# Last expert feed-forward of a four-layer block: from all experts for every token to blocks of tokens sorted by expert

## What is computed

```
h = xn * rsqrt(mean(xn * xn) + eps) * norm_w          # xn is the layer norm of x
logits = h @ gate_w.T + gate_b
vals, idx = top_k(logits, 2);  wts = softmax(vals)
t1 = einsum('td,efd->tef', h, mlp1_w) + mlp1_b        # 8 experts, 2 x 128 columns each
glu = min(t1[..., ::2], 7);  lin = clip(t1[..., 1::2], -7, 7)
act = glu * sigmoid(1.702 * glu) * (lin + 1)
y = einsum('tei,edi->ted', act, mlp2_w) + mlp2_b
out = xn + sum over the 2 chosen experts of y * wts
x = x + tanh(g_ffn[3]) * out
```

## Time and profile before

| | us |
|---|---|
| three runs | 1872.49, 1875.36, 1875.47 (median 1875.36) |
| the profiled execution, its own time | 1866.39 |
| its span, first to last instruction | 1864.6 |
| `feed_forward3`: from the last tile of the last attention (1595.3) to the end of the span | 269.3 |
| busy over the span: PE / DVE / ACT / POOL | 1517.3 / 1345.4 / 780.6 / 642.2 |
| mean granted TensorE clock | 0.918 |

### The profile page before, as it was taken

The page is one execution under the profiler, slowest core; times in us unless marked ns, Lnnn a source line. Parts: engine busy times, 40 slices in busy tenths (PEclk is TensorE's granted clock), DMA queues, the critical chain, the costliest instruction groups (busy, mean ns, idle before and its releaser), DMA issues. The chain is left out here.

```text
span 1864.6 us, 33511 instructions
## 1 busy us (share of the span) xinstructions
PE 1517.3 (81%) x10824; PEld 920.6 (49%) x10824; DVE 1345.4 (72%) x3512; ACT 780.6 (42%) x1314; POOL 642.2 (34%) x649
## 2 busy tenths in 40 slices
PE   3788885378989799889889898944789899778877
PEld 1455453145555465555555555522355556445444
DVE  5667776666566537888888888876565656698998
ACT  1555563145656423333333433421356556333333
POOL 0223220012221003353444453454123220477786
PEclk9989997589999899999999999975989999798999
DMA  7543540244344000000000000003053432000000
GB/s 171 68 70 47 73 63 1 34 136 74 48 62 62 1 1 1 7 1 7 6 1 6 0 7 18 1 0 74 0 75 46 67 52 36 1 1 12 11 12 12
DMA packets 62835, 63.59 MB, mean 34 GB/s; under 512 B 6065, under 2 KB 57777, under 8 KB 62129
## 3 DMA queue, kind: packets, MB, share of 16 engines
q1 hardware_dynamic: 62704, 61.99, 20.3%
HBM read 22.12 MB, written 2.10 MB: 13 GB/s over the span
## 5 line engine op out<-in xcount | busy, mean ns | idle before, releaser
L1225 DVE TENSOR_REDUCE neg_max<-bank 128x4 f32<-128x512 f32 x384 | 259.5, 687 | 128.9 <-PE bank L856 126.8
L670 ACT ACTIVATE probs<-bank 128x512 f32<-128x512 f32 x384 | 229.1, 597 | 239.1 <-PE bank L879 236.8
L1026 PEld LDWEIGHTS bank<-room,area 128*128 128x128 f32 x2048 | 249.4, 196 | 100.0 <-issue 62.9
L1026 PE MATMUL bank<-room,area 128*128 128x128 f32 x2048 | 259.8, 281 | 32.0 <-DVE area L1499 18.3
L746 ACT ACTIVATE work<-bank 128x512 f32<-128x512 f32 (+1 forms) x192 | 114.5, 596 | 355.0 <-PE bank L1051 349.9
L439 POOL TENSOR_SCALAR rstd_a<-meanvar 128x4 f32<-128x4 f32 x64 | 16.9, 265 | 676.8 <-DVE meanvar L1181 676.8
L854 PE MATMUL bank<-mask_b,ident_b 128*128 128x512 bf16 x384 | 159.4, 415 | 70.5 <-DVE neg_max L1225 56.7
L1055 PE MATMUL bank<-xT,room 128*128 128x512 f32 (+1 forms) x384 | 200.6, 605 | 15.7 <-DVE area L1499 15.5
L1051 PE MATMUL bank<-xT,room 128*128 128x512 f32 (+1 forms) x384 | 198.4, 599 | 0.0
L1499 DVE TENSOR_TENSOR area<-work,bank 128x512 f32<-128x512 f32 (+1 forms) x192 | 128.8, 679 | 94.5 <-PE bank L1055 74.4
L568 POOL TENSOR_TENSOR prod<-mask_i,work 128x128 f32<-128x128 f32 (+3 forms) x128 | 126.4, 1020 | 154.6 <-DVE mask_i L1560 154.6
(11 more groups left out here) (167 smaller groups left out, 2481.9 us busy)
## 6 DMA issues: line engine op xcount, KB each, us to landing
q_rows<-area SPq DMA_DIRECT2D x144, 128.0 KB
k_rows<-area SPq DMA_DIRECT2D x288, 64.0 KB
ctxT<-ctx_t SPq DMA_DIRECT2D x24, 256.0 KB, 7.7
mask_i<-mask SPq DMA_DIRECT2D x8, 256.0 KB, 8.6
work<-ctx_in SPq DMA_DIRECT2D x8, 256.0 KB, 2.8
out<-x SPq DMA_DIRECT2D x4, 512.0 KB, 3.2
room<-w_down SPq DMA_DIRECT2D x1, 1536.0 KB, 13.4
room<-w_gate SPq DMA_DIRECT2D x1, 1408.0 KB, 6.3
```

The costliest lines, as they stand in the source:

```text
L670: act.activation(probs[j].rearrange("p a b -> p (a b)"), T_BANK[j % 2][:], ACT.Exp).then_inc(exp_done, 1)
L1026: mm = pe.matmul(dst[:, t * P:(t + 1) * P], h[:, t * P:(t + 1) * P], w, start=i == 0, stop=i == len(terms) - 1)
L1225: dve.tensor_reduce(neg_max[:, 4 * j:4 * j + 4], S_BANK[j % 2][:].rearrange("p (h k) -> p h k", h=4), AX.X, ALU.max, negate=True).then_inc ...
```

## The change

The 32 tiles are taken as 4 chunks (`NCH`) of 8 tiles (`TC`), 1024 tokens. Each token of a chunk has two rows, one for each chosen expert. Its two rows are written to a region of the DRAM tensor `moe_rows`, sorted by expert, each expert starting at a multiple of 128 rows; a region has 24 blocks of 128 rows, since 2048 rows of 8 experts need at most 23. Then the blocks are processed, four at a time (`QUAD`), so 6 steps a chunk and 24 in all, numbered k below. Each block has one expert.

- **DVE** per chunk: `choose(c)` (13 small operations: the two experts of each of 8 tiles) and `put(c)` (19: the row number of each token and the expert of each block, as integers, and the two weights). PE counts in between, in `ranks(c)`: 17 bf16 matmuls with a triangle and with ones.
- **POOL** per chunk: 16 indirect transfers of 128 rows of 512 bytes out of `h_all` to `moe_rows` (`scatter`, 8 for each half chunk) and 16 back (`gather`) into `y_taken`. The products move to DVE, `h` too (it is kept for all 32 tiles, `h_all`).
- **SP** loads step k with one transfer of four blocks at a fixed address (`load`, four buffers) and stores the result over it (`store`). It clears `moe_rows` before `token_attention`, in 4 transfers of 1.5 MB.
- **PE** per step: turn the four blocks, multiply by the expert's `mlp1`, whose column in `room` comes from a register (`value_load`, one number for four experts, then shifts), add the bias by a second matmul of a one-hot column with the bias in three bf16 parts, turn the product, multiply by `mlp2` in the same way.
- **DVE** per step: two clamps from PSUM and a product (`gated`), a second product after the sigmoid (`hide`). Per chunk, `combine3` adds the 16 gathered tiles to `x`, times their weights.
- **ACT** per step: copy the turned blocks, the sigmoid, copy the turned product, copy the result.
- At the start one more 64 KB constant is loaded and cast. `load_experts3` loads the biases after the last token attention, since they lie in its buffer.

The core of the diff:

```diff
+TC = 2 * TG
+NCH = NT // TC
+QUAD = 4
+NQ = 6
 ...
             def load_experts3():
                 sp.wait_ge(x_written, NT * 4)
                 sp.dma_start(wr3[:], gate3).then_inc(experts_loaded, 16)
 ...
+                sp.wait_ge(tok_written, NT)
+                sp.dma_start(bias_f[BIAS_ROWS], bias3).then_inc(experts_loaded, 16)
+
+            def feed_forward3():
 ...
+                def load(k):
+                    if k % NQ == 0:
+                        sp.wait_ge(scattered[k // NQ], 16 * 2 * TC)
+                    if k >= 4:
+                        sp.wait_ge(blk_turned, k - 3)
+                    waits_apart(sp)
+                    sp.dma_start(blk[k % 4], moe_rows[k * GT:(k + 1) * GT].rearrange("(j p) d -> p j d", p=P)
+                                 ).then_inc(blk_loaded[k % 4], 16)
 ...
+                for k in range(NCH * NQ):
+                    load(k)
+                    if k >= 4:
+                        store(k - 4)
 ...
+                def scatter(c, half):
+
+                    pool.wait_ge(placed, c + 1)
+                    pool.wait_ge(h3_ready, 2 * c + half + 1)
 ...
+                    for t in range(TG):
+                        for k in range(2):
+                            o = 2 * (TG * half + t) + k
+                            pool.indirect_dma_start(
+                                moe_rows, bass.IndirectOffsetOnAxis(place_i[:, c, o:o + 1].bitcast(mybir.dt.uint32), 0),
+                                h_all[:, TC * c + TG * half + t, :], None).then_inc(scattered[c], 16)
+
+                def gather(c):
+
+                    for b in range(2):
+                        pool.wait_ge(blk_stored[b], 16 * NQ // 2 * (c + 1))
+                    if c >= 2:
+                        pool.wait_ge(combined, c - 1)
 ...
+                for c in range(3):
+                    scatter(c, 0)
+                    rms_norm(2 * c + 3)
+                    scatter(c, 1)
+                    if c < 2:
+                        rms_norm(2 * c + 4)
+                gather(0)
+                scatter(3, 0)
+                scatter(3, 1)
+                for c in range(1, NCH):
+                    gather(c)
 ...
+                    four = pe.value_load(expert_i[0:1, c, q:q + 1], min_val=0, max_val=E ** QUAD - 1)
+                    for j in range(QUAD):
+                        weights_at[k, j] = pe.snap(((four >> 3 * j) & (E - 1)) * (3 * P))
 ...
+                for k in range(NCH * NQ):
+                    c, q = divmod(k, NQ)
+                    turns = min(2 * c + 4 + (q >= 2) + (q >= 4), 2 * NCH)
+                    if k + 1 < NCH * NQ:
+                        turn_blk(k + 1, turns if q < NQ - 1 else min(2 * c + 6, 2 * NCH))
+                    up(k)
+                    if c < 2 and q in (1, 3):
+                        turned(2 * c + 4 + (q == 3), k + 2)
+                    if k >= 1:
+                        turn_hidden(k - 1)
+                    if k >= 2:
+                        down_blk(k - 2)
+                    if c < 2:
+                        if q == 3:
+                            logits(c + 2)
+                        if q == 5:
+                            ranks(c + 2)
 ...
+                for k in range(NCH * NQ):
+                    c, q = divmod(k, NQ)
+                    gated(k)
+                    if c < 2:
+                        if q == 0:
+                            group_norm(2 * c + 5)
+                        if q == 1 and c == 0:
+                            group_stats(6)
+                        if q == 4:
+                            choose(c + 2)
+                        if q == 5:
+                            put(c + 2)
+                            if c == 0:
+                                group_norm(6)
+                                group_stats(7)
+                    hide(k)
+                    if c >= 2 and q == NQ - 1:
+                        combine3(c - 2)
+                combine3(2)
+                combine3(3)
```

More of the change, by code:

```diff
@@ new lines, in program @@
+        chosen = small((2 * TC + 1) * E, BF16).rearrange("p (o e) -> p o e", e=E)
+        rank = small(2 * TC * E).rearrange("p (o e) -> p o e", e=E)
+        place = small(2 * TC)
+        place_i = small(NCH * 2 * TC, I32).rearrange("p (c o) -> p c o", c=NCH)
+        weight = small(NCH * 2 * TC).rearrange("p (c k t) -> p c k t", c=NCH, k=2)
+        blocks_of, ends, begins = small(E), small(E), small(E)
+        blocks_i = small(E, I32)
+        below = small(E * E).rearrange("p (e f) -> p e f", e=E)
@@ L513, in feed_forward3 @@
-                rms_norm(0)
-                def body(gp, first, last):
-                    for gr, b, is_first, left in groups(gp, first, last):
-                        for e in range(E):
-                            if e >= 1:
-                                hide(E * gr + e - 1, e - 1, DB3 + 9 * gr + e - (1 if e >= 3 else 2))
-                            elif not is_first:
-                                hide(E * gr - 1, 7, DB3 + 9 * gr - 2)
-                            if e == 1 and left >= 1:
-                                rms_norm(gr + 1)
-                            products(E * gr + e, e)
@@ L1607, in norm_apply, with group_stats, group_norm @@
+                def group_stats(p):
+                    norm_stats(p, NT * 5 + TG * (p + 1))
+                def group_norm(p):
                     norm(p, 56 + p)
                     dve.wait_ge(xn_ready, XN3 + p + 1)
[L1609 to L1613 removed]
```

481 lines of the change are left out of this document (334 added, 147 removed).

## The result

The changed kernel takes 1921.2 us (median of 4 runs, 1918.3 to 1924.7), the kernel before 1873.9 us beside it (4 runs, 1863.6 to 1875.5): a ratio of 1.0265, with an interval of 1.0237 to 1.0294. It is slower by 47 us, where 12 us less were forecast.

A forecast was written before the change was run, and what follows sets the result against it. DVE was taken to bound the last stage, PE close behind. Seven terms along the chain through DRAM summed to 257.3 us against 269.3, 12.0 less, so 1863.4 us for the median; range 1838 to 1932.

The forecast's parts named there:

- 1, to the first scatter: Last stage's start until the first chunk's row numbers: statistics, norms, logits, `choose`, `ranks`, `put`; 26.0 us.
- 2, scatters, landing, load: First chunk's sixteen scatters (20.3 us) with a 3.65 norm between halves, landing 2.15, load 2.9; 29.1 us.
- 3, first step: First expert step, from turning the blocks to `hide(0)`, including DVE's norm waiting for 1/std on POOL; 13.8 us.
- 4, the other 23 steps: Steps at PE's 5.86 us each (134.8), plus 10.0 other PE work and 8 delays, less 4.4; 148.4 us.
- 5, out and stored: After the last `hide`: turn, copy, down products, copy (5.0 us) and the store (3.0); 8.0 us.
- 6, last gather: Last chunk's 16 indirect transfers and a 2.15 us landing, with nothing beside them; 22.6 us.
- 7, combine, store: Last `combine3` of 16 tiles (5.6 us), and from the last tile to the end 3.8; 9.4 us.
- T: POOL's time for one indirect transfer, 128 of them; taken as 1.27 us, bounds 0.37 and 2.13, called the weakest number.
- Registers: PE's value read and register instructions, 0.3 us a step; rival 1.1 a step, 3 us slower than before, chance 0.12.
- The lock: POOL and DVE blocking each other: some 10 us exposed, or, if descriptor writing is blocked, T 3.1, stage 195 us longer.
- The queue as the bound: Rival: GpSimd's in-order transfer queue bounds the last stage; gain gone from 1.49 us a transfer, 71 us more at 2.13; chance 0.34.
- Costed at nothing: Clearing `moe_rows`, the extra constant and bias load hidden; if uncovered, clearing some 38 us, bias 2 to 3.

The follow-up runs named there:

- e10: The changed kernel unedited, as control beside three edited kernels on one chip; 1851.5 us, ratio 0.989 to the kernel before.
- e1: Changed kernel with TensorE's expert weights at addresses fixed in the program, without value load and register arithmetic; 1854.1 us, ratio 0.992 to the kernel before.
- e3: Changed kernel with GpSimd pauses: one pow after each transfer of gather 1, four after every fourth of gather 2; 1888.7 us.
- e9: Changed kernel with pauses in gather 2 only, four pows on GpSimd after every fourth transfer; 1866.6 us.
- e4: Kernel before with 32 indirect scatters from GpSimd's queue added in the second feed-forward's first group, to rows nobody reads; 1874.0 us.
- e5: The changed kernel run once more without edit; 1923.8 us, ratio 1.028 to the kernel before.
- e7: Changed kernel with 52 products of 128x4 added behind GpSimd's last gather; 1868.7 us.
- e13: Changed kernel with 26 small matmuls added behind TensorE's last one; 1854.1 us, ratio 0.991 to the kernel before.
- e6: Changed kernel with 96 empty instructions behind GpSimd's last one, which did not lengthen the executed program; 1925.6 us, ratio 1.029 to the kernel before.
- e14: Changed kernel with 32 scatters added in the second feed-forward, fixed weight addresses in steps 12 to 15, and gather 1 as plain transfers; 1944.4 us.
- e15: Changed kernel with three GpSimd series added: 32 indirect transfers back to back, 16 indirect with a pause each, 64 plain; 1966.4 us.
- e16: Changed kernel with GpSimd pausing about 4.4 us after every eighth indirect transfer, chunk 2's scatters to gather 1; 1905.3 us, ratio 1.019 to the kernel before.
- e17: Changed kernel with GpSimd pausing about 2.2 us after every fourth indirect transfer, chunk 2's scatters to gather 2; 1896.4 us, ratio 1.0143 to the kernel before.
- e18: The changed kernel unedited, as control on the same chip beside the kernel with pauses after every fourth transfer; 1926.8 us, ratio 1.0295 to the kernel before.

## Why the prediction was right or wrong

The terms of the sum, each from the rows that end it: the forecast, the control without stalls (e10, stage from 1606.1 us), and the execution first measured (stage from 1601.8 us; both starts are 1.5 us ahead of GpSimd's first operation of the stage, as in the earlier trace rows):

| term | forecast | e10 | first measured |
|---|---|---|---|
| 1, to the first scatter | 26.0 | 25.8 | 25.8 |
| 2, scatters, landing, load | 29.1 | 28.9 | 29.1 |
| 3, first step | 13.8 | 15.6 | 16.5 |
| 4, the other 23 steps | 148.4 | 140.7 | **205.5** |
| 5, out and stored | 8.0 | 8.2 | 8.2 |
| 6, last gather | 22.6 | 21.4 | 21.3 |
| 7, combine, store | 9.4 | 8.3 | 8.3 |
| stage | 257.3 | 248.9 | 314.7 |

**What failed is term 4.** The forecast took the work of PE, DVE and ACT in a step as untouched by what GpSimd does beside it, except where they wait for its result ("PE is the engine of a step, DVE, ACT (2.6) and SP lie beside it"). Without stalls that holds: the last two chunks go at 5.44 us a step (L1885 from 1753.75 to 1813.54 in 11 steps), 0.4 under the forecast, and the stage is 8 us shorter than forecast. With stalls the same 23 steps take 205.5 us in place of 148.4, 57 more than forecast, and this is the whole difference in sign: all three engines of a step start late beside GpSimd's series with their operands ready. The list of what would show it wrong did not hold this form; neither did any rival.

**T.** 1.27 forecast, 1.26 measured. The number was right by luck: it was taken from a product over 128 partitions, and what was measured is 0.95 us and a gap of 0.30, of which a plain transfer takes 0.53. The bounds held as well, the lower one nearly as a price: a plain transfer costs GpSimd 0.53 against SP's 0.37. The queue's waits were forecast at 38.9 and are 36.5 in e10 (25.4 for row numbers, 11.1 for stores).

**Registers.** 0.3 us a step was too much, if anything. With fixed addresses (e1) the last 11 steps took 5.25 us each, in e10 5.44; but e3, which has the registers, took 5.26, so not even that difference is shown. In total e1 was no faster (ratio 0.992 against 0.989). The floor of 0.6 us for a read, cited from the Trainium skill, DMA: Bandwidth & Descriptors, section Latency and other measured facts, doesn't show here: in e10 TensorE waits 1.2 us for issue at L1273 in the whole stage, three times, 0.5 at most. The forecast's prices were also off by its own sum: over 23 steps, 0.6 us would have left 5 us of the gain (not 6), and 1.1 us would have made the kernel 6 us slower (not 3).

**The lock.** No transfer ran as long as the forecast feared: the longest scatter took 1.59 us, so the 3.1 us that the Trainium skill's SBUF — State Buffer, section SBUF: two separate sides, would give for blocked descriptor writing did not come in this mix of VectorE work. What came went the other way: not GpSimd waiting for an engine, but TensorE, VectorE and ScalarE waiting while GpSimd issues.

**The queue as the bound** was the rival with a chance of 0.34, and the side that was measured was slower, but not by it: GpSimd waits 98 us in the measured stage. That the queue can bound is seen where pauses lengthen it: with those of e9 the last gather starts at 1835.27 in place of 1825.19 (e10), and the span ends 10.1 us later as well.

**Costed at nothing.** The stages ahead were to stay as they are. They did not quite stay: the token attention's last step stands at 1304.3 us in the measured execution and at 1307.2 in e10, against 1298.6. From 690 to 1000 us, where the engines compute the same as before, the clock is 0.96 in both and 0.99 in the kernel before. The kernel before with 32 scatters added (e4) has GpSimd's first operation of the last stage at 1606.0 too, against 1596.8, so part of it is likely the one execution of before that was shown; that was not tried apart. In e10's profiled execution the stage starts 10.8 us later than in that one, which leaves about 10 of the 20.4 us that the stage gains; by the medians 18.7 are left.

So the mechanism of the gain was right and its size too small (18.7 us measured beside e10, 12 forecast), and the sign of the first measurement comes from an effect that the trace of the kernel before can't show.

**What stays open.** What differs between an occasion with stalls and one without. It isn't the program (e5 and e10 are the same), nor the chip (6 and 8 showed both), and it held for all kernels and executions of one occasion: those of e1 to e3, e7 to e9 and e10 to e13 without, those of the first measurement, e5 and e6, e14, e15 and e16, e17 and e18 with. The kernel before took 1864 to 1877 us on all of them. Whether it is where the program and its tensors lie in memory, or something outside the program, no run tested. How the three engines' starts are held up was seen only as time. One guess is that their instructions are brought too late. The page has two queues that bring them (packets, MB, share); the larger one:

```profile
q8 instruction: 73, 1.20, 0.3%
```

That is 16 KB a packet. The Trainium skill, Advanced Engine Details and Errata, section ISA Cache, says the same: lines of 16 KB, 256 instructions each, and this queue's packets agree (those of the other, q14, are of 8 KB). If that is so, a late line should show as one long gap in 256 instructions; the measured delays stand at nearly every product. And from 1737 to 1752 us, in the middle of the first stall, neither queue moves a packet. Both speak against this form of the guess, and no run tested another.

## What to carry to other kernels

A long unbroken series of indirect transfers on GpSimd's queue can hold up the starts of TensorE, VectorE and ScalarE, though nothing in the program links them; keep such a series to four or so beside work that counts, with a pause, or put it where the other engines are idle, and give the queue the room for the pauses first. A wait for "issue" on an engine whose operands are ready is a sign to look at what the other queues do in that stretch, not at its own code. So is a wait whose releaser had long been done: look up when the operand was complete before you call one engine the victim of another. And a run without its control beside it on the same occasion is no evidence: three edits in a row seemed to remove a stall that was not there.

## What the hardware showed that I had not expected

- An indirect transfer of 128 rows of 512 bytes costs GpSimd 0.95 us and a gap of 0.30, a plain one of the same size 0.53 in all.
- Beside a series of them TensorE's weight loads and products started 0.7, 1.4 or 2.1 us after one another, in whole steps of about 0.70 us (1737.98, 1738.68, 1739.38 and 1741.48 in the timeline above), from the 7th to 10th transfer on and until 2 to 4 us after the end of the series.
- VectorE and ScalarE were held up by up to 15 us (in e18 up to 22) at operations whose operands TensorE had completed, earlier in the series than TensorE itself, and then often started within 0.05 us of one of TensorE's late starts.
- A transfer every 2.5 us did not do it to TensorE, nor did 64 plain transfers in 34 us; bursts of four with 2.2 us of pause left starts up to 2.7 us late, bursts of eight with 4.4 us up to 5.8.
- The same program had this or hadn't, by occasion: medians of 1851.5, or 1921 to 1927 us. The kernel before, which has no indirect transfer, did not show two levels.
